# A fused two-layer network on one core: the first feed-forward's down product with w2 held still

## The reference, cut to what matters

```python
gate_scores = xf @ gate_w.T
top1 = jnp.argmax(jax.nn.softmax(gate_scores, axis=-1), axis=-1)
one_hot = jax.nn.one_hot(top1, N_ROUTING, dtype=xf.dtype)
masked = xf[None, :, :] * one_hot.T[:, :, None]
h = jax.nn.relu(jnp.einsum('end,edh->enh', masked, w1) + b1[:, None, :])
expert_out = jnp.einsum('enh,ehd->end', h, w2) + b2[:, None, :]
shared = jax.nn.relu(xf @ sw1 + sb1) @ sw2 + sb2
return expert_out.sum(axis=0) + shared
...
x = _layernorm(x + _L0_ffn_ref(x, ...), axis=-1)
```

## Time and profile before

| what | us |
|---|---|
| median of 3 runs | 635.62 |
| lowest, highest | 633.32, 635.85 |
| profiled execution, its own time | 635.56 |
| its span | 633.7 |
| TensorE, VectorE busy in the span | 576.3 (91%), 404.8 (64%) |
| ScalarE, GpSimd busy | 266.4 (42%), 226.7 (36%) |

### The profile page before, as it was taken

The page is one execution under the profiler, slowest core; times in us unless marked ns, Lnnn a source line. Parts: engine busy times, 40 slices in busy tenths (PEclk is TensorE's granted clock), DMA queues, the critical chain, the costliest instruction groups (busy, mean ns, idle before and its releaser), DMA issues.

```text
span 633.7 us, 11896 instructions
## 1 busy us (share of the span) xinstructions
PE 576.3 (91%) x4428; PEld 447.1 (71%) x4428; DVE 404.8 (64%) x1057; ACT 266.4 (42%) x531; POOL 226.7 (36%) x327
## 2 busy tenths in 40 slices
PE   3899999999987799999789999999889999999994
PEld 3657667766756599899556666665558888888883
DVE  2477877787764733554657788877246666666655
ACT  3586755575630322220055555555632222222220
POOL 2264545554320535363735555554510000000000
PEclk9699999999978999999959999999869999999999
DMA  5953131223000600002221221220000000000000
GB/s 208 324 197 122 69 134 67 102 100 125 10 1 0 252 1 1 1 2 68 70 74 49 63 63 48 68 73 4 4 1 0 2 1 18 1 18 2 1 18 17
DMA packets 25352, 37.64 MB, mean 59 GB/s; under 512 B 3536, under 2 KB 15568, under 8 KB 24912
## 3 DMA queue, kind: packets, MB, share of 16 engines
q1 hardware_dynamic: 25296, 36.89, 17.5%
HBM read 10.01 MB, written 1.05 MB: 17 GB/s over the span
## 4 chain that ended last, share of the span: by engine, by line
PE 63%; DVE 18%; issue 8%; ACT 3%; POOL 3%; DMA 2%; SPq 2%; POOLq 0%; DVEq 0%; ACTq 0%
PE f_O L1611 7%; PE f_O L801 6%; PE f_H L59 5%; PE f_H L61 5%; PE f_H L60 5%; PE a_MI L485 5%; DVE a_UA L366 4%; PE a_S L1328 4%; PE a_Y L437 4%; PE a_YP L1357 3%; PE a_S L1336 3%; PE a_PJ L59 2%; DVE a_m L1172 2%; PE a_S L423 2%; DVE a_rr L357 2%
## 5 line engine op out<-in xcount | busy, mean ns | idle before, releaser
L226 POOL TENSOR_TENSOR a_Y<-a_Y 128x256 f32<-128x256 f32 x64 | 59.5, 933 | 97.0 <-ACT a_Y L265 97.0
L366 DVE SCALAR_TENSOR_TENSOR a_UA<-a_UA,a_mask 128x768 f32<-128x768 f32 x64 | 68.3, 1075 | 27.1 <-ACT a_UA L273 26.6
L1172 DVE TENSOR_REDUCE a_m<-a_S 128x3 f32<-128x384 f32 x117 | 63.7, 554 | 31.6 <-PE a_S L1336 26.5
L1479 ACT ACTIVATE f_sg<-f_H 128x512 f32<-128x512 f32 x64 | 38.2, 597 | 103.1 <-PE f_H L61 103.1
L1557 DVE TENSOR_TENSOR f_hid<-f_H,f_sg 128x512 f32<-128x512 f32 x64 | 44.3, 692 | 53.2 <-PE f_H L61 43.1
L273 ACT ACTIVATE a_UA<-a_S,a_one 128x768 f32<-128x768 f32 x64 | 57.6, 900 | 44.8 <-PE a_S L424 44.6
L1096 POOL TENSOR_SCALAR_AFFINE_SELECT f_w<-f_w 128x256 f32<-128x256 f32 x128 | 51.8, 407 | 67.9 <-ACT f_w L1143 67.7
L1143 ACT ACTIVATE f_w<-a_ST 128x384 f32<-128x384 f32 x118 | 56.9, 493 | 39.7 <-PE a_ST L1334 39.7
L1611 PEld LDWEIGHTS f_O<-f_w,f_hid 128*128 128x128 f32 x512 | 65.9, 191 | 8.1 <-issue 3.3
L1611 PE MATMUL f_O<-f_w,f_hid 128*128 128x128 f32 x512 | 67.8, 276 | 2.0 <-DVE f_acc L1535 2.0
L437 PE MATMUL a_Y<-a_UA,a_V 128*64 128x256 f32 (+1 forms) x512 | 58.4, 351 | 0.0
(11 more groups left out here) (282 smaller groups left out, 1390.0 us busy)
## 6 DMA issues: line engine op xcount, KB each, us to landing
a_q<-a_c_h SPq DMA_DIRECT2D x16, 256.0 KB, 2.5
a_q<-a_c_l SPq DMA_DIRECT2D x16, 256.0 KB, 2.6
a_k<-a_c_h SPq DMA_DIRECT2D x16, 256.0 KB, 2.5
a_k<-a_c_l SPq DMA_DIRECT2D x16, 256.0 KB, 2.6
f_w<-in_f_w SPq DMA_DIRECT2D x1, 2048.0 KB, 8.8
a_q<-a_c_h SPq DMA_DIRECT2D x16, 128.0 KB
a_q<-a_c_l SPq DMA_DIRECT2D x16, 128.0 KB
a_k<-a_c_h SPq DMA_DIRECT2D x16, 128.0 KB
```

The lines of the kernel that those rows point to most:

```text
L226: pool.tensor_tensor(Y2[:, v % 2, j, :], Y[:, v % 2, j, :], Y[:, v % 2, j, :], ALU.mult).then_inc(y2_ready, 1)
L366: dve.scalar_tensor_tensor(UA[:, j % 4, :, :], UA[:, j % 4, :, :], 1.0, mask[:, None, :].to_broadcast([P, 2, SW]), ALU.add, ALU.mult).then ...
L1172: dve.tensor_reduce(m3[:, b % 2, h % H1, :], s_bank(h)[:, 0:SW].rearrange("p (a n) -> p a n", a=3), AX.X, ALU.max).then_inc(max_done, 1)
```

## The change

In blocks 0 to 2 the down product has w2's chunk as the stationary operand and the hidden chunk of 512 tokens moving, so the output has features on the partitions. An even chunk is one f32 matmul; an odd chunk is split by VectorE in two operations into high and low parts and multiplied in three f32r passes. VectorE's odd chunk becomes max(x, -b) instead of max(x + b, 0), and the difference, w2 times b summed over the odd chunks, is a vector that TensorE computes first (`cv_ready`), ScalarE copies and adds when it takes the output from PSUM to `oT`. TensorE turns that by four transposes into bank T[1] (`turn`), which VectorE's residual reads. w2's high part is one cast on VectorE at the start of the stage, its low part three subtractions after VectorE's first three odd chunks. In block 3 the orientation is the old one, but chunk by chunk. The down product now runs three chunks behind the up product (LAG) instead of a block. `residual(i)` moves from chunk 1 of block i+2 to chunk 7 of block i+1, `finish(i)` from chunk 7 to chunk 3 of block i+2, both earlier; block 2's `finish` stands before block 3's residual.

```diff
@@ -590,6 +590,7 @@
     NC = NE0 * HC
+    LAG = 3
     ctx = ExitStack()
@@ -607,7 +608,12 @@
                 parts[1][e] = sb(f"f0_x{name}1{e}", [P, BT], F32R)[:, :]
-        hid = sb("f0_hid", [P, 2, NC, BT])
+        hid, odd = sb("f0_hid", [P, 3, BT]), sb("f0_odd", [P, 3, BT])
+        act_h, act_l = sb("f0_act_h", [P, 3, BT], F32R), sb("f0_act_l", [P, 3, BT], F32R)
+        w2_h, w2_l = sb("f0_w2_h", [P, NC, D], F32R), sb("f0_w2_l", [P, NC, D], F32R)
+        neg_b = sb("f0_negb", [P, NC])
+        c_vec = sb("f0_cvec", [P, 1])
+        oT = sb("f0_oT", [P, BT])
 
@@ -624,7 +630,8 @@
         h_act, h_dve = sem("h_act"), sem("h_dve")
-        o_ready = sem("o_ready")
+        d_ready, oT_ready, o_ready = sem("d_ready"), sem("oT_ready"), sem("o_ready")
+        cv_ready, cv_read, w2_split, high_step = sem("cv_ready"), sem("cv_read"), sem("w2_split"), sem("high_step")
         res_ready, ln_step, var_ready, rstd_ready = (sem(n) for n in "res_ready ln_step var_ready rstd_ready".split())
@@ -699,12 +706,24 @@
 
+            def turn(i):
+                act.wait_ge(d_ready, (i + 1) * NC)
+                if i >= 1:
+                    act.wait_ge(o_ready, i)
+                act.activation(oT[:, :], O[i % 2][:, :], ACT.Identity, bias=c_vec[:, 0:1]).then_inc(oT_ready, 1)
+
+            act.wait_ge(cv_ready, 1)
+            act.activation(c_vec[:, :], G[:, 64:65], ACT.Copy).then_inc(cv_read, 1)
+            act.wait_ge(cv_read, 1)
             for i in range(NBLK):
                 for c in range(0, NC, 2):
-                    act.wait_ge(h_ready, i * NC + c + 1)
-                    if i >= 2 and c == 0:
-                        act.wait_ge(o_ready, i - 1)
-                    act.activation(hid[:, i % 2, c, :], HP[(i * NC + c) % 3][:, :], ACT.Relu, bias=b1[:, c:c + 1]).then_inc(h_act, 1)
+                    n = i * NC + c
+                    if i >= 1 and c == 4:
+                        turn(i - 1)
+                    act.wait_ge(h_ready, n + 1)
+                    if n >= 6:
+                        act.wait_ge(d_ready, n - 5)
+                    act.activation(hid[:, n // 2 % 3, :], HP[n % 3][:, :], ACT.Relu, bias=b1[:, c:c + 1]).then_inc(h_act, 1)
                     if i + 1 < NBLK and c in (2, 8):
@@ -720,6 +739,14 @@
             dve.wait_ge(*before)
+            dve.tensor_scalar(neg_b[:, :], b1[:, :], -1.0, None, ALU.mult)
+            dve.tensor_copy(w2_h[:, :, :], w2[:, :, :]).then_inc(w2_split, 1)
+            dve.wait_ge(w2_split, 1)
+
+            def split_low(third):
+                cs = slice(4 * third, 4 * third + 4)
+                dve.tensor_tensor(w2_l[:, cs, :], w2[:, cs, :], w2_h[:, cs, :].bitcast(F32), ALU.subtract).then_inc(w2_split, 1)
+
             def prepare(i, part):
@@ -728,11 +755,15 @@
             def residual(i):
-                dve.wait_ge(o_ready, i + 1)
+                if i < NBLK - 1:
+                    dve.wait_ge(o_ready, i + 1)
+                else:
+                    dve.wait_ge(d_ready, NBLK * NC)
                 dve.wait_ge(xb_ready, i + 1)
...
                     dve.wait_ge(mem["w_split"], NE0 + 1)
-                dve.tensor_tensor(res[i % 2], O[i % 2][:, :].rearrange("p (t d) -> p t d", t=TB), xb[:, i % 2, :, :], ALU.add).then_inc(res_ready, 1)
+                total = T[1] if i < NBLK - 1 else O[i % 2]
+                dve.tensor_tensor(res[i % 2], total[:, :].rearrange("p (t d) -> p t d", t=TB), xb[:, i % 2, :, :], ALU.add).then_inc(res_ready, 1)
                 dve.wait_ge(res_ready, i + 1)
@@ -740,11 +771,21 @@
 
-            for i in range(NBLK + 1):
+            for i in range(NBLK):
                 for c in range(1, NC, 2):
-                    if i < NBLK:
-                        dve.wait_ge(h_ready, i * NC + c + 1)
-                        dve.tensor_scalar(hid[:, i % 2, c, :], HP[(i * NC + c) % 3][:, :], b1[:, c:c + 1], 0.0, ALU.add, ALU.max).then_inc(h_dve, 1)
+                    n = i * NC + c
+                    dve.wait_ge(h_ready, n + 1)
+                    if n >= 6:
+                        dve.wait_ge(d_ready, n - 5)
+                    high, low = act_h[:, n // 2 % 3, :], act_l[:, n // 2 % 3, :]
+                    if i < NBLK - 1:
+                        dve.tensor_scalar(high, HP[n % 3][:, :], neg_b[:, c:c + 1], None, ALU.max).then_inc(high_step, 1)
+                        dve.wait_ge(high_step, n // 2 + 1)
+                        dve.scalar_tensor_tensor(low, HP[n % 3][:, :], neg_b[:, c:c + 1], high.bitcast(F32), ALU.max, ALU.subtract).then_inc(h_dve, 1)
+                    else:
+                        dve.tensor_scalar(odd[:, n // 2 % 3, :], HP[n % 3][:, :], b1[:, c:c + 1], 0.0, ALU.add, ALU.max).then_inc(h_dve, 1)
+                    if i == 0 and c < 6:
+                        split_low(c // 2)
                     if i + 1 < NBLK and c in (3, 9):
@@ -755,10 +796,11 @@
                             prep_rotate(dve, mem, b, k - 1, (T[1], G)[k - 1])
-                    if c == 1 and i >= 2:
-                        residual(i - 2)
-                    if c == 7 and i >= 2:
+                    if c == 3 and i >= 2:
                         finish(i - 2)
+                    if c == 7 and i >= 1:
+                        residual(i - 1)
+            finish(NBLK - 2)
             residual(NBLK - 1)
@@ -772,9 +814,12 @@
                 elif part == 1:
+                    pe.wait_ge(cv_read, 1)
                     gate_scores(pe, mem, i, xT, G)
...
                     pe.wait_ge(xl_ready, 2 * i)
+                    if i >= 2:
+                        pe.wait_ge(res_ready, i - 1)
                     gate_transpose_x0(pe, mem, i, T[1])
@@ -789,26 +834,48 @@
 
-            def down(i, s):
-
-                t, third = divmod(s, 3)
-                if s == 0 and i >= 2:
-                    pe.wait_ge(res_ready, i - 1)
-                if s < 3:
-                    pe.wait_ge(h_act, i * NC // 2 + 2 * (third + 1))
-                    pe.wait_ge(h_dve, i * NC // 2 + 2 * (third + 1))
-                for c in range(4 * third, 4 * third + 4):
-                    k = pe.matmul(O[i % 2][:, t * D:(t + 1) * D], hid[:, i % 2, c, t * P:(t + 1) * P], w2[:, c, :],
-                                  start=(c == 0), stop=(c == NC - 1))
-                if s == NC - 1:
-                    k.then_inc(o_ready, 1)
-
-            for i in range(NBLK + 1):
+            def down(n):
+                i, c = divmod(n, NC)
+                if c == 0 and i >= 2:
+                    pe.wait_ge(oT_ready, i - 1)
+                out, start, stop = O[i % 2][:, :], c == 0, c == NC - 1
+                if i == NBLK - 1:
+                    pe.wait_ge((h_act, h_dve)[c % 2], n // 2 + 1)
+                    act = hid[:, n // 2 % 3, :] if c % 2 == 0 else odd[:, n // 2 % 3, :]
+                    for t in range(TB):
+                        k = pe.matmul(O[i % 2][:, t * D:(t + 1) * D], act[:, t * P:(t + 1) * P], w2[:, c, :],
+                                      start=(start and t == 0), stop=stop, skip_group_check=True)
+                elif c % 2 == 0:
+                    pe.wait_ge(h_act, n // 2 + 1)
+                    k = pe.matmul(out, w2[:, c, :], hid[:, n // 2 % 3, :], start=start, stop=stop)
+                else:
+                    pe.wait_ge(h_dve, n // 2 + 1)
+                    if i == 0 and c % 4 == 1:
+                        pe.wait_ge(w2_split, c // 4 + 2)
+                    high, low = act_h[:, n // 2 % 3, :], act_l[:, n // 2 % 3, :]
+                    pe.matmul(out, w2_h[:, c, :], high, start=start, stop=False)
+                    pe.matmul(out, w2_l[:, c, :], high, start=False, stop=False)
+                    k = pe.matmul(out, w2_h[:, c, :], low, start=False, stop=stop)
+                k.then_inc(d_ready, 1)
+
+            def turn(i):
+                pe.wait_ge(oT_ready, i + 1)
+                if i == NBLK - 2:
+                    pe.wait_ge(mem["rb_ready"], 1)
+                for t in range(TB):
+                    k = pe.transpose(T[1][:, t * P:(t + 1) * P], oT[:, t * P:(t + 1) * P], mem["ident"][:, :])
+                k.then_inc(o_ready, 1)
+
+            for c in range(1, NC, 2):
+                k = pe.matmul(G[:, 64:65], w2[:, c, :], b1[:, c:c + 1], start=(c == 1), stop=(c == NC - 1))
+            k.then_inc(cv_ready, 1)
+            for i in range(NBLK):
                 for c in range(NC):
-                    if i < NBLK:
-                        up(i, c)
-                    if i >= 1:
-                        down(i - 1, c)
+                    up(i, c)
+                    if i * NC + c >= LAG:
+                        down(i * NC + c - LAG)
+                    if i >= 1 and c == 6:
+                        turn(i - 1)
                     if i + 1 < NBLK and c in (2, 5, 8):
@@ -828,7 +895,11 @@
                                 pe.wait_ge(mem["rb_ready"], 2 * (b - 1) + k)
+                                if k == 1:
+                                    pe.wait_ge(res_ready, NBLK - 1)
```

(2 more changed lines are left out.)

## The result

The changed kernel takes 639.21 us (median of 6 runs, 633.99 to 642.37), the kernel before on the same chip 634.24 (6 runs, 632.35 to 635.85): a ratio of 1.0075, 95% interval 1.0044 to 1.0105. That is 4.8 us more, slower by over 0.5%. Every ratio in this document leaves out the runs that the chip made in a second, slower state (none of these twelve), so it need not equal the quotient of two medians. The profiled execution of after took 642.37 us with a span of 640.6, against 635.56 and 633.7, so it is at the slow end of its runs. Its 6.9 us of span must be split before they are explained.

What follows compares the result with a forecast made beforehand. VectorE's queue was to stretch block 0 and GpSimd's chain to set the stage's end: +3.5 for that chain and +0.4 for the clock, +3.9 on 635.56, gave 639.5 us, range 633.5 to 644.

Steps and rivals of the forecast that it cites:

- GpSimd's chain: End of the stage: GpSimd's queue moves +6.6, less 3.1 of slack, so block 3's pow and the end come +3.5 us.
- the clock: Stage opening: idle TensorE may fall to half clock, +0.4 us added, bounds 0 and 3.4.
- Prices on TensorE: Down product: an even chunk costs 0.86 us, an odd chunk three passes, 0.70, against 0.89 for an old chunk.
- fifth rival: Even down chunks: the 512-column f32 matmul costs 1.0 us or more, +2.4, giving 641.9 us; chance 0.05.
- Block 0: First block of the stage: ends at 230.0 instead of 222.0, +8.0 us, bounds +6.7 (no hold-up anywhere) and +12.
- VectorE's chain: Block 0: VectorE's old and new operations in sequence, with chunk 5 done at 223.65, limit the block.
- a low third beside a memset: Block 0: w2's first low third, 0.69 us, may be held up by GpSimd's memsets; taken as 0.9.
- TensorE as block 0's only limit: Block 0: were TensorE the only limit, it would end at 224.5, a shift of +2.5 us.
- third rival: VectorE's additions fit into block 0, shift +2.5, no waits in blocks 1 and 2: -4.1, 631.5 us; chance 0.13.
- Blocks 1 and 2: Middle blocks: shifts of -0.6 and -0.4 us, so block 3 starts 7.0 later.
- TensorE's end: Block 3: 15 down chunks instead of 24, -8.0 us, against a start 7.0 later, so TensorE ends -1.0.
- Everything behind moves with it.: After block 3's pow: last normalisation, memsets, copies and attention hang on it and move with it, +3.5 us.

Runs made afterwards that it cites:

- order_only: The changed kernel with the old orientation in all four blocks, so only the order is new, no split of w2, no turn; ratio to before 1.0035.
- a_pow: The changed kernel with GpSimd's power for block 3 taken ahead of the second batch's low parts; ratio to before 1.0002.
- order_early: The changed kernel with the old orientation in all four blocks and GpSimd's weight splits moved out of the last block; ratio to before 0.9977.
- f32: The changed kernel with odd chunks of blocks 0 to 2 in full float32, without VectorE's pair, split of w2 or bias vector; ratio to before 1.0039.
- a_tail: The changed kernel with filling matmuls that nobody reads in TensorE's short waits at attention 1's end; ratio to before 0.9976.
- b_tail: The kernel before with filling matmuls that nobody reads in TensorE's short waits at attention 1's end; ratio to before 0.9963.
- a_early: The changed kernel with GpSimd's weight splits moved out of the last block, into blocks 1 and 2; ratio to before 1.0055.
- a_fill: The changed kernel with 36 matmuls that nobody reads ahead of four TensorE waits in attention 1's opening; ratio to before 1.0060.

## Why the forecast was right, and where it was not

The forecast was 639.5 us, slower by over 0.5% as the likeliest case; measured were 639.21. The sum was +3.9, in the form +3.5 for GpSimd's chain and +0.4 for the clock. In the profile it is +2.9 up to steady and +2.3 behind it, besides 1.7 of scatter ahead of the stage. So the number is better than its parts. Taken step by step:

- **Prices on TensorE.** Even chunk 0.86 forecast, 0.86 measured. Odd passes 0.23 each, as forecast. The fifth rival (a dearer float32 matmul) is out.
- **Block 0: +8.0 forecast, +6.7 measured**, the bound I gave for no hold-up anywhere. VectorE's chain was as drawn: cast 0.95 (0.96), second operation of the pair 0.75 (0.75), chunk 5's pair done at 224.23, which is 14.2 behind L336 where I had 223.65 less 208.31, 15.3. Two terms were mis-sized: the cast didn't wait for GpSimd's add (0.45), and the 0.9 that I added for a low third beside a memset was nothing, it took 0.71 while the memset of 216.01 ran. The Trainium skill (SBUF — State Buffer, "SBUF: two separate sides"), which lets only a GpSimd operation that reads SBUF hold up such a subtraction, was right here. By it the forecast would have been 7.1 for the block. Some 0.5 of this lead was lost again, since TensorE at half clock came to the scores 0.62 late. That VectorE is the block's limit is only half right: the wait it causes ends at 216.05, and when chunk 5's pair is done, TensorE is busy with the matmuls ahead of the ninth up chunk until 224.37.
- **TensorE as block 0's only limit: +2.5 in the third rival.** order_only has neither pair nor split, and still +4.6 with a wait of 2.01 for VectorE's first odd chunk. The rival was too generous by 2 us. The fast case of 631.5 wasn't to be had with this order alone.
- **Blocks 1 and 2: -0.6 and -0.4 forecast, -0.75 and -0.44 measured.** The wait in block 2 is there, 0.97 for VectorE. Block 3 starts +5.5 and not +7.0, all of it from block 0.
- **TensorE's end: -1.0 forecast, variance -2.2 measured.** The 1.5 us of block 3's start account for it.
- **GpSimd's chain: power +3.5 forecast, +1.5 measured.** The mechanism is shown, by the row at 303.79 and by a_pow, order_only and order_early. Of the 2.0 us too many, 1.5 are block 3's start. The 0.5 that are left are covered by SyncE's copies of the first batch: the kernel before has a long issue there (the group at 286.52 takes 1.98), the changed one has not (1.23 at 293.56), which my shift of the whole chain carried along.
- **"Everything behind moves with it."** This step failed. From power to steady it is 23.6 us before and 25.1 after. SyncE's issues explain 1.1 of the 1.4: a group of two takes 2.29 instead of 1.22. All five kernels with the split of w2 show such a group in this opening (1.94 to 2.39) and none of the nine others, so it came with the change; the late power is not the reason, since a_pow's is early and its issue is slow (2.12). In each of the five the long issue overlaps the 16 KB transfer of instructions, which starts 100.7 to 101.9 us after L336's product; in the nine others no such transfer falls among these issues. Over all 14 traces 49 of the 64 issues of these copies that take over 0.9 us overlap one, and 62 of the 1728 shorter ones. So a fetch of instructions, moved into the issues by the change's other number of instructions, is the likely cause; no run tests it.
- **The clock: +0.4 forecast.** The fall in block 0 that I feared is there (215.8 to 219.2, after the idle 2.58 us). I had it lie partly beside VectorE's chain; TensorE waits nowhere from there to block 1, and by the estimate under f32 it cost 1.1 to 1.5 us of block 0's 6.7. By the Trainium skill (TensorE: Matmul & The Clock Gate, "Part 1: The HAM clock gate"), taken alone, it was to be +1.7, which is nearer. The other part I hadn't looked for: a fall 230 us later, in code that nobody touched, was 24 us long instead of 17, and the rest is 2.3 us longer. a_tail against b_tail shows that half clock there is the cause of that part: without it the changed kernel's rest is no longer than before's. By the ratios the fillers won 4.0 us more in the changed kernel than in before, so 2.3 may be too low. Why the clock falls for longer is open: a_early, a_pow and a_fill run the same code there and have 6.8 us of it in their profiles.

That the total came out right is luck. In the profile, 2.0 too much for the power, 1.4 too little behind it and 1.9 too little for the clock leave 1.3 too little (+5.2 against +3.9). By the medians the loss was 5.0, and 639.5 met 639.21 because before's six runs have 634.24, 1.3 under the 635.56 that I added to. The range held.

## What to carry to other kernels

A gain on the busiest engine is real only as far as the in-order queues behind it let it through: here 4.65 us of TensorE gave 0.4 at the next stage's steady start until GpSimd's splits were moved. Ask which instruction stands in front of the one that ends the stage, on every engine. Look for half clock where TensorE is busy, not where it idles: 46 matmuls that nobody reads, in the short waits just ahead of such a stretch, were worth 2.3 to 6.3 us, and 36 where TensorE waits anyway were worth nothing that shows. And before reading a difference of a few us, measure from an instruction that both kernels share; 1.7 of the 6.9 us here arose before the changed code began.
